# The first projections of a four-part network in three float32r products a tile, with the layer norm folded into the q weights

## The reference

```
n = layernorm(x)                      # (x - mean) / sqrt(var + 1e-5), over 512
q = rms_norm(n @ q_w.T + q_b) * norm_q_w
k = rms_norm(ctx @ k_img_w.T + k_img_b) * norm_k_img_w
v = ctx @ v_img_w.T + v_img_b
x = x + attention(q, k, v) @ o_w.T + o_b      # 16 heads of 32
```

## Time and profile before

| | |
|---|---|
| three timed runs | 1653.78, 1659.73, 1667.11 us; median 1659.73 |
| the profiled execution | 1676.87 us, span 1675.0 us |
| TensorE busy in the span | 1470.4 us, 88% |
| VectorE, ScalarE, GpSimd busy | 61%, 52%, 38% |
| mean granted TensorE clock | 0.938 |

### The profile page before, as it was taken

The page is one execution under the profiler, slowest core; times in us unless marked ns, Lnnn a source line. Parts: engine busy times, 40 slices in busy tenths (PEclk is TensorE's granted clock), DMA queues, the critical chain, the costliest instruction groups (busy, mean ns, idle before and its releaser), DMA issues. The chain is left out here.

```text
span 1675.0 us, 37963 instructions
## 1 busy us (share of the span) xinstructions
PE 1470.4 (88%) x8537; PEld 1170.0 (70%) x8538; DVE 1026.8 (61%) x2055; ACT 869.5 (52%) x1988; POOL 630.1 (38%) x717
## 2 busy tenths in 40 slices
PE   2999989999884399999999999999981579999999
PEld 1545555665672298888888888888871468888888
DVE  3343446787568757667677666666634456667732
ACT  0222247888337556666666666666640234444442
POOL 2212136777114232232223323222316476666322
PEclk9999968999995599999999999999995789999999
DMA  5000079000117158877877777777637444444200
GB/s 225 25 19 25 19 275 359 2 1 2 48 57 295 44 166 280 276 270 261 277 268 266 270 263 248 263 252 263 221 109 251 130 148 134 138 135 135 81 13 26
DMA packets 90247, 273.83 MB, mean 163 GB/s; under 512 B 12421, under 2 KB 12550, under 8 KB 88966
## 3 DMA queue, kind: packets, MB, share of 16 engines
q1 hardware_dynamic: 66070, 191.80, 32.5%
q0 software_dynamic: 23680, 77.61, 15.4%
q10 hardware_dynamic: 432, 3.67, 0.5%
HBM read 204.88 MB, written 76.81 MB: 168 GB/s over the span
## 5 line engine op out<-in xcount | busy, mean ns | idle before, releaser
L974 POOL DMA_INDIRECT xg<-h_rows,idx x168 | 184.8, 1100 | 463.6 <-PE m_x L1002 454.4
L1017 PE MATMUL m_g<-wgu_high,bxTh 128*128 x660 | 236.2, 358 | 2.2 <-DVE bxTl L1090 2.1
L1017 PE MATMUL m_g<-wgu_low,bxTh 128*128 x660 | 223.5, 339 | 0.0
L1017 PE MATMUL m_g<-wgu_high,bxTl 128*128 x660 | 223.3, 338 | 0.0
L1420 PE MATMUL f_g<-x4T_high,ffn_gu 128*128 128x256 f32 x704 | 176.5, 292 | 14.5 <-issue 12.2
L1420 PE MATMUL f_g<-x4T_low,ffn_gu 128*128 128x256 f32 x704 | 169.3, 282 | 0.0
L1090 DVE TENSOR_TENSOR bxTl<-m_x,bxTh 128x512 fp32r<-128x512 f32 x166 | 114.8, 692 | 84.6 <-ACT bxTh L1159 64.2
L852 DVE TENSOR_TENSOR wgu_low<-raw_gu,wgu_high x61 | 107.3, 1759 | 82.9 <-ACT wgu_high L842 81.7
L1311 POOL DMA_INDIRECT G<-y_rows,slot x128 | 135.3, 1057 | 56.6 <-issue 50.5
L415 POOL TENSOR_TENSOR prob<-prob,inv 128x512 f32<-128x512 f32 x128 | 130.5, 1041 | 62.8 <-DVE inv L366 62.8
L1177 ACT ACTIVATE y<-m_y 128x512 f32<-128x512 f32 x164 | 98.3, 600 | 105.9 <-PE m_y L1037 91.1
(11 more groups left out here) (240 smaller groups left out, 3222.4 us busy)
## 6 DMA issues: line engine op xcount, KB each, us to landing
raw_gu<-in_exp_gu SPq DMA_DIRECT2D x64, 768.0 KB, 6.8
y_rows<-y SPq DMA_DIRECT2D x164, 256.0 KB
raw_d<-in_exp_d SPq DMA_DIRECT2D x64, 512.0 KB, 7.7
y_rows<-zero SPq DMA_DIRECT2D x64, 256.0 KB, 3.5
ffn_gu<-ffn_gu_words SPq DMA_DIRECT2D x1, 5632.0 KB
X<-in_x SPq DMA_DIRECT2D x4, 1024.0 KB, 17.8
ctxT<-in_ctxT SPq DMA_DIRECT2D x16, 256.0 KB, 2.6
h_rows<-h SPq DMA_DIRECT2D x16, 256.0 KB, 2.0
```

The source lines that it names most:

```text
L974: eng.indirect_dma_start(xg[:, u, :].bitcast(F32), None, h_dram, bass.IndirectOffsetOnAxis(ap=idx[half][:, u:u + 1], axis=0)).then_inc(s_g ...
L1017: m = eng.matmul(pg[u % 2][:, 0:2 * I], xT[l][:, u % 2, c, :], W.gu[r][:, buf * DC + c, :], start=c == 0 and n == 0, stop=c == DC - 1 and ...
```

## The change

`project` is written anew; `attend` gets a list of semaphores that SyncE clears at its start, behind its first transfer. What is done differently:

- Each product is three float32r matmuls for each of 4 chunks: eight of the high part of the tile with high and low weights, then four of the low part with high weights. ScalarE makes high parts (a copy into float32r), VectorE low parts (a subtraction), for 12 chunks of weights once and for context and x of each tile.
- x comes transposed from memory (`xT`, laid out on the host beside x, as the context is), so that `xn`, its transposes and the `xnT` copy are gone. The mean is taken out of the q weights instead: `mean_w` (all 1/512) times the q weights gives each column's mean (4 float32 matmuls, `pq[1]`), and `centred` subtracts it. rstd is applied behind the product: q = product x rstd + bias.
- The weight row of k is multiplied into that of q (`w_row`), so k is scaled by its inverse root alone; this moves from VectorE to ScalarE.
- Bias sums stay in PSUM (`pk`, `pq` are written in place), squares go to PSUM.
- X arrives in four parts during the loop; statistics of tile t are taken in slot t + 1. GpSimd forms rstd by a power and adds the bias row in place.
- The loop is unrolled into slots: in slot s stand k and v of tile s, the turn of k of tile s, q of tile s - 2 (`LAG`) and the turn of q of tile s - 3 (`TURN`).

```diff
-            with eng.Fori(0, NT // 2) as i:
...
-                        m = eng.transpose(pxT[:, bass.ts(c, P)], xn[:, par, bass.ts(c, P)], ident[:, :])
...
-                            m = eng.matmul(psum[:, :], lhs[:, par, c, :], W[:, w, c, :], start=c == 0, stop=c == DC - 1)
...
+            def products(psum, high, low, w, first, ready):
+                for c in range(DC):
+                    if first:
+                        eng.wait_ge(s_low, ORDER.index(w) * DC + c + 1)
+                    for n, r in enumerate((Wh, Wl)):
+                        eng.matmul(psum[:, :], high[:, c, :], r[:, w, c, :], start=c == 0 and n == 0, stop=False)
+                ready()
+                for c in range(DC):
+                    m = eng.matmul(psum[:, :], low[:, c, :], Wh[:, w, c, :], start=False, stop=c == DC - 1)
+                return m
...
+            for s in range(NT):
+                k(s)
+                if s >= TURN:
+                    turn_q(s - TURN)
+                v(s)
+                if s == 0:
+
+                    eng.wait_ge(s_mean_w, 1)
                     for c in range(DC):
...
+                        eng.wait_ge(s_w[0][c], 16)
+                        m = eng.matmul(pq[1][:, :], mean_w[:, :], raw_w[:, 0, c, :], start=c == 0, stop=c == DC - 1)
+                    m.then_inc(s_mean, 1)
+                    eng.wait_ge(s_id, 2)
+                turn_k(s)
+                if s >= LAG:
+                    q(s - LAG)
+            q(NT - 2)
+            turn_q(NT - 3)
+            q(NT - 1)
+            turn_q(NT - 2)
+            turn_q(NT - 1)
...
+            for s in range(NT + TURN):
+                if s >= TURN:
+                    deviation(actQ, s - TURN, dveQ, "qb", pq[(s - TURN) % 2][:, :], qms)
+                if s == NT:
+                    tokens(NT - 2)
+                    tokens(NT - 1)
+                if s >= TURN:
+                    turned(actQT, s - TURN, peQT, "qT", qT, pqT)
+                if s < NT:
+                    deviation(actK, s, dveK, "kb", pk[:, :], kms)
+                if LAG <= s < NT:
+                    tokens(s - LAG)
+                if s < NT:
+                    dveK.wait(eng, s, "kr")
+                    peKT.wait(eng, s - 1, "kT")
+                    actK.done(eng.activation(kn, pk[:, :], ACT.Copy, scale=krs[:, 0:1]), "kn")
...
+            def q_scaled(t):
+                peQ.wait(eng, t, "q")
+                poolR.wait(eng, t, "rstd")
+                dveQ.done(eng.scalar_tensor_tensor(pq[t % 2][:, :], pq[t % 2][:, :], rstd[:, t:t + 1], q_row, ALU.mult, ALU.add), "qb")
+
+            def q_normed(t):
+                actQ.wait(eng, t, "sd")
+                dveQ.done(eng.reciprocal(qrs[:, :], qms[:, 1:2]), "qr")
+                dveQ.wait(eng, t, "qr")
+                peQT.wait(eng, t - 1, "qT")
+                dveQ.done(eng.scalar_tensor_tensor(qn, pq[t % 2][:, :], qrs[:, 0:1], w_row[:, :], ALU.mult, ALU.mult), "qn")
...
+                if s >= TURN:
+                    q_scaled(s - TURN)
+                    q_normed(s - TURN)
+                if s < NT:
+                    k_bias(s)
+                    k_scale(s)
...
+                if LAG <= s < NT:
+                    tokens(s - LAG)
...
+                if s < NT:
+                    v_bias(s)
...
+                if s + 1 < NT:
+                    context(s + 1)
+                if 1 <= s <= NT:
+                    moments(s - 1)
```

More of the change, by code:

```diff
@@ L114, in project @@
[L114 to L117, removed]
+        with ExitStack() as arriving:
+            raw_w, raw_c, raw_x = [arriving.enter_context(nc.sbuf_tensor(f"raw_{n}", [P, k, DC, w], F32)) for n, k, w in (("w", 3, D), ("c", CBUF, P), ("x", 1, P))]
@@ L132, in _ @@
[L132 to L153, removed]
@@ new lines, in _ @@
+            context(0)
+            for c in range(DC):
+                eng.dma_start(raw_w[:, 2, c, :], wT_in[2][:, c, :]).then_inc(s_w[2][c], 16)
+            context(1)
+            residual(0)
+            for t in tiles:
+                if t + CBUF < NT:
+                    context(t + CBUF)
+                if t % 4 == 1 and t + 3 < NT:
+                    residual(t // 4 + 1)
+                if t < NT - 1:
+                    tokens(t)
+                if t == NT - 3:
+                    tokens(NT - 1)
@@ L161, in _ @@
                               pattern=[[-1, P]], channel_multiplier=1).then_inc(s_id, 1)
[L162 to L175, removed]
+            eng.memset(minus_half[:, :], -0.5).then_inc(s_eps, 1)
@@ new lines, in _ @@
+            eng.memset(eps[:, :], RMS_EPS).then_inc(s_eps, 1)
+            eng.wait_ge(s_eps, 2)
+            eng.wait_ge(s_rows, 96)
+            for t in tiles:
+                dveS.wait(eng, t, "mv")
+                poolR.done(eng.tensor_scalar_add(rstd[:, t:t + 1], mv[:, t % 2, 1:2], LN_EPS), "var")
+                poolR.wait(eng, t, "var")
+                poolR.done(eng.tensor_tensor(rstd[:, t:t + 1], rstd[:, t:t + 1], minus_half[:, :], ALU.pow), "rstd")
+                eng.tensor_tensor(X[:, t, :], X[:, t, :], o_row, ALU.add)
@@ new lines, in k, with v, q @@
+            def k(t):
+                actC.wait(eng, t, "high")
+                actK.wait(eng, t - 1, "kn")
+                peK.done(products(pk, ch[:, t % CBUF, :, :], cl[:, t % CBUF, :, :], 1, t == 0, lambda: dveC.wait(eng, t, "low")), "k")
+            def v(t):
+                dveV.wait(eng, t - 1, "vb")
+                peV.done(products(pv, ch[:, t % CBUF, :, :], cl[:, t % CBUF, :, :], 2, t == 0, lambda: None), "v")
+            def q(t):
+                actX.wait(eng, t, "high")
+                dveQ.wait(eng, t - 2, "qn")
+                peQ.done(products(pq[t % 2], x_at(t, xh, ch), x_at(t, xl, cl), 0, t == 0, lambda: dveX.wait(eng, t, "low")), "q")
@@ new lines, in turn_k, with turn_q @@
+            def turn_k(t):
+                actK.wait(eng, t, "kn")
+                actKT.wait(eng, t - 1, "kT")
+                for c in range(DC):
+                    m = eng.transpose(pkT[:, bass.ts(c, P)], kn[:, bass.ts(c, P)], ident[:, :])
+                peKT.done(m, "kT")
+            def turn_q(t):
+                dveQ.wait(eng, t, "qn")
+                actQT.wait(eng, t - 1, "qT")
+                for c in range(DC):
+                    m = eng.transpose(pqT[:, bass.ts(c, P)], qn[:, bass.ts(c, P)], ident[:, :])
+                peQT.done(m, "qT")
@@ L249, in attend, with context, tokens @@
-def attend(nc, a, qT, kT, V, Wraw, Wo, ident, y_dram, ffn_gu, ffn_d):
+            for x in (dveC, dveX, dveV, dveK, dveQ, dveS):
+                x.start(eng)
+            def context(t):
+                actC.wait(eng, t, "high")
+                dveC.done(eng.tensor_tensor(cl[:, t % CBUF, :, :], raw_c[:, t % CBUF, :, :], ch[:, t % CBUF, :, :].bitcast(F32), ALU.subtract), "low")
+            def tokens(t):
+                actX.wait(eng, t, "high")
+                dveX.done(eng.tensor_tensor(x_at(t, xl, cl), x_at(t, raw_x, raw_c), x_at(t, xh, ch).bitcast(F32), ALU.subtract), "low")
```

215 lines of the change are left out of this document (128 added, 87 removed).

## The result

| | before | changed |
|---|---|---|
| median of the timed runs | 1659.89 us | 1633.52 us |
| range | 1653.78 to 1667.11 | 1629.46 to 1635.14 |
| profiled execution, span | 1675.0 us | 1632.5 us |
| projections end, us from the start | 219.9 | 186.6 |

The ratio is 0.9835, with an interval of 0.9802 to 0.9868: 27 us less (22 to 33); the medians themselves differ by 26. The forecast was 1626 (1605 to 1649), 34 us off the median.

What follows compares the result with a forecast made beforehand. TensorE was taken to bound the projections; 45 us to slot 3, 13 steps of 9.8 and 13.4 at the end gave 186 against 219.9 us. Taking 34 us off the 1659.73 median gave 1626 us, range 1605 to 1649.

Steps and rivals of the forecast that it cites:

- What bounds the kernel: Projections: TensorE alone sets the pace; later stages keep their instructions and move forward by the stage's gain, 34 us.
- The product: Projection loop: twelve float32r matmuls 0.229 us apart take 2.75 us, or 2.83 behind transposes, instead of 3.43.
- The chain and the step: Projection loop: q's and k's normalisation through other engines makes TensorE wait 0.65 us per slot, 9.8 us in all.
- TensorE's floor: Projection loop: three products and two transpose groups without waits, 9.13 us; as a rival 1617 us, 0.18 with shorter cold attention.
- VectorE 1 us from being late: Projection loop: VectorE finishes its operations before q arrives at 10.0 us, with 1 us of slack.
- PSUM written in place at no cost: Bias operations that read and write PSUM: nothing added, with 0.3 us a slot allowed against.
- The start: Beginning of projections: loads, weight conversions and first products put the beginning of slot 3 at 45 us (42 to 49).
- the price of the means: Beginning of projections: q weights' means and centring cost about 10 us, for taking layer norm out of the loop.
- The end: Last projections: late x for q(14), two products and turn, q(15)'s uncovered chain, turn and copy take 13.4 us.
- The sum: Projections: 45 + 13 x 9.8 + 13.4 ends them at 186 us against 219.9, 34 us less.
- The clock: Rival in the projection loop: TensorE's waits bring half clock, 86 us more, some 1712 us; chance 0.06 for part or all.
- Attention's stretch at half clock: Rival in attention: half clock, some 37 us before, has no fixed end; over 50 us more gives 1641 to 1693, chance 0.05.

Runs made afterwards that it cites:

- the third trace: The changed kernel run once more, unaltered: 1631.69 us, ratio 0.9806; projections end at 185.4 us.
- The padded kernel: Changed kernel plus 55 chained ScalarE copies behind the projections' last slot, about 34 us with TensorE idle: 1663.07 us, ratio 1.0004.
- the version with the better start: Changed kernel with second context converted ahead of q weights, and x of tile 14 loaded into the buffer v(15) frees: 1634.78 us, ratio 0.9799.

## Why the prediction was right

*What bounds the kernel, and that the gain moves all later stages forward.* Right, as far as the scatter tells: the rest took 1446.6 us before and 1445.4 after in the mean of the traces, which scatter over 14 and 10 us.

*The product.* 2.75 and 2.83 us; measured 2.73 (v of tile 0, which follows k without transposes, from 17.59 to 20.32) and 2.83 (109.61 to 112.44), so 0.228 us a matmul in the first. The Trainium skill (TensorE: Matmul & The Clock Gate, Back-to-back issue gap) gives some 0.131; these rows are far from it. The experiment with the old product had the step at 11.17 us, by the same reckoning 11.2.

*The chain and the step.* 9.8 us; measured 9.66. Of the two waits, 0.4 and 0.25, there were 0.31 and 0.12, and a turn took 0.42 instead of 0.36 us: 2.73 + 0.31 + 0.42 + 2.83 + 0.12 + 0.42 + 2.83. That it is a closed chain was right: an edit that delayed qn by 0.46 us made the step 0.46 longer. With kn ahead of the high part of x it gained 0.06, since TensorE waited for kn by only 0.12. The step lies 0.4 us above TensorE's floor, which by these durations is 9.23.

*VectorE 1 us from being late, PSUM written in place at no cost.* Right: 1.11 us of wait for q, 0.76 and 0.70 us for the operations that write PSUM, against 0.75 and 0.69.

*The start.* Step 3 at 45, measured 44.78. But the price of the means was mis-sized: some 10 us in the text, 1.5 to 1.9 at step 3 in the experiment without them. The text gives no terms for the 10. Without the means, ScalarE's second table load (1.28 us), the wait for the bias rows (1.66) and the conversions of the q weights and of the second context still stand there. The forecast did not hang on this price, only on the 45.

*The end.* 13.4 us from the last step's end; measured 16.1 (170.5 to 186.6). The two waits were there, 3.31 and 2.60 us. x for q(14) came 3.5 us late instead of 2.7; the two products and the turn took 7.7 us instead of 6.0, since some seven of q(14)'s matmuls started 0.43 us apart; and the last turn and copy took 1.8 instead of 1.3, again at half clock. The sum had no half clock at the end. In the third trace, where q(14) ran at full clock, the end took 14.7 us.

*The sum.* 186 us for the stage against 186.6, so 33 us gained where 34 were forecast. That it is so close is partly luck: thirteen steps were 1.8 us shorter than forecast and the end 2.7 us longer, and the end itself, mostly by the clock, differs by 2 us among the three traces. The median moved by 26, 28 and 31 us in three measurements, whose intervals share 0.9818 to 0.9832, 28 to 30 us. That is 3 to 5 us short of the stage's gain. The padded kernel excludes a cost of 5 us in the way the projections end and attention starts, and leaves one of up to 3 open; the traces show none, with a scatter of 5 to 7 us either way. Whether the 3 to 5 us are noise or a loss stays open.

*The rivals.* The clock did not fall in the loop. It fell at both ends and cost a few us there, so the rival's mechanism is real in this kernel. Behind the wait of 3.3 us for k(1) it was at half in all three traces, behind the same wait for q(14) in two of three, and the last turn behind 2.60 us was at half in two of three. The page that was cited for it, of small idle times between groups of matmuls that make the clock swing (the Trainium skill, TensorE: Matmul & The Clock Gate, A second HAM failure mode: psum-queue depth-cycling), is not borne out for waits of 0.1 to 0.3 us twice in 9.7: the granted clock was 1.00 from 40 to 170 us. Attention's stretch at half clock was as loose as its rival had it, 19 to 45 us in sum, with no bias from the change that these traces show. The 37 us that the prediction took from one trace, and made a sign of being wrong, is thus no property of the kernel.

## What to carry to other kernels

When a stage is bound by TensorE and another stage of the same kernel already runs the new form of matmul, the spacing of starts there gives the new floor to 1%; then follow one step through all queues for the chain that the shorter products no longer cover. Look at the first and last steps by themselves: there the covers are missing, and a wait of some 3 us of TensorE may be paid twice, once as idle time and once as half clock behind it. Whether it is can change from one execution to the next of the same kernel. When an operation is put into a chain to test it, read from the rows by how much it really delayed the next one before comparing with the step. And measure how much the untouched stages scatter from one execution to the next before explaining a few us that are missing.

## What the runs showed of the hardware

- Behind a wait of 3.3 us, k(1) had seven or more of its matmuls of 128x512 about 0.43 us apart in all three traces of the changed kernel, and later ones 0.229. Behind 3.3 to 3.5 us, q(14) had the same in two of them, and none in the third. Behind 1.97 us (kn(1) in the version with the better start) the granted clock stayed full; in the kernel without the means it fell after a wait of 2.20 us, four transposes and most of a wait of 1.76 us (1.00 from 22 to 24 us, 0.56 from 24 to 26, first matmul at 25.30).
- In the changed kernel's first trace the first product of the execution, k(0), took 5.1 us at a granted clock that reads 1.00, against 2.73 and 2.83 for later ones.
- The half clock in attention summed to 19, 32, 41 and 41 us in four executions of one and the same kernel, with the same work, and of the rest's scatter of 14 us it explains up to 9 (194.4 us from the first scores to routing with 19 us of it, 203.4 with 41).
- A VectorE operation of 128x512 (0.68 us by itself) put between a reciprocal and the operation that waits for it delayed the latter by 0.46 us.
- ScalarE's scaled copy out of PSUM took 0.67 us where the plain copy took 0.60.
